# Region attention on one core: where a region's two evacuations of turned probabilities and its first turn stand in the order of ScalarE and TensorE

## The chip, the cores and the metric

The kernel runs on one core of one Trainium2 chip. The metric is device time in microseconds (us), the median of several runs. The core has TensorE (PE, which multiplies and turns matrices and writes to PSUM), ScalarE (ACT), VectorE (DVE), GpSimd (POOL) and SyncE (SP, which issues DMAs). Each engine works through its own instructions in order, and semaphores join them.

## What is computed

The input is a batch of 8 images of 56x56 tokens with 256 channels, f32. After a group norm, a 1x1 projection gives queries, keys and values. Each image is cut into 7x7 = 49 regions of 64 tokens. Each region chooses 4 regions by the product of mean queries and mean keys, and attends to their 256 keys with 8 heads of 32 channels. A depthwise 3x3 convolution of the values is added, a 1x1 projection follows, and the input is added.

```python
qkv = einsum('nchw,oc->nohw', group_norm(x), qkv_w) + qkv_b
a_r = pool(q) @ pool(k)                 # 49 x 49 for each image
idx = top_k(a_r, 4)                     # four key regions for each query region
attn = softmax(q * 256**-0.5 @ gathered_k.T)   # 8 heads, 64 queries, 256 keys
out = attn @ gathered_v + depthwise3x3(v)
y = x + (einsum(out, out_w) + out_b)
```

## The kernel before

**The loop.** After a start of 89 us that projects the first image, the loop runs over 56 rows of regions (`s`, 7 rows an image) and the 7 regions of a row (`rc`); `r = 7 s + rc` numbers 392 regions. Every engine has its own copy of this loop with its own order, written by hand. Beside the attention of the present regions, a row's seven passes carry the projections of the row seven rows later (values `v`, keys `k`), of queries two rows later, the turned values (`vt`), the output projection of the row before, the 16 taps of the convolution on VectorE, and the statistics of an image two ahead. The last seven rows have no `v`, `k` and `vt` left to project. The first row of an image also chooses its regions, and the last row of an image also settles a later image's statistics.

**One region.** It goes through these steps; the eight heads are four slices of PSUM (`u` = 0 to 3), with two heads on the two halves of the partitions.

- `scores` (PE, L907 to L920): 16 matmuls on tiles of 32x64 into `s_bank`, one bank for each `u`. There is one set of these four banks, so the scores of the next region wait until all four exponentials of this one are done.
- `maximum` (DVE, L697): two reductions, each over two banks.
- `exp` (ACT, L495): four activations into `probs`, of which there is one copy. Exponentials 0 and 1 of a region wait for the first turn of the region before, 2 and 3 for its second.
- `turn_probs(r, 0)` and `turn_probs(r, 1)` (PE, L923): four transposes each, of two slices, into `pt_bank`. This is one bank, so each turn waits until the last one was evacuated.
- `probs_t_out(r, 0)` and `(r, 1)` (ACT, L504): the two evacuations of `pt_bank` to `probs_t`, a copy of 128x512 each.
- `attend` (PE, L935): 32 matmuls on tiles of 128x32 with the selected values. It waits for both evacuations of its region.
- `turn_recips` (PE, L952), `recips_out` (ACT, L510), `normalize_o` (DVE, L713), `take_region` (POOL, L332): the sums' reciprocals are turned and evacuated, the result is scaled and added to the convolution.

**The order on TensorE in pass `r`** (L990 on): first turn of `r`; wait for the exponentials of `r`; the image's small matmuls where there are any; scores of `r + 1`; attend of `r - 1`; second turn of `r`; projections; `turn_recips(r)`; more projections.

**The order on ScalarE in pass `r`** (L537 on): first evacuation of `r`; one or two evacuations of the row's projections (`q_out`, `v_out`, `k_out`, `vt_out`), called the row's evacuations here; exponentials 0 and 1 of `r + 1`; second evacuation of `r`; exponentials 2 and 3 of `r + 1`; `recips_out(r)`.

```python
pe.wait_ge(probs_t_evac, 2 * r + hf)            # turn_probs: the bank is free
act.wait_ge(probs_turned, 2 * r + hf + 1)       # probs_t_out: the turn is done
act.wait_ge(probs_turned, 2 * (r - 1) + u // 2 + 1)   # exp, u = 0 and 2
pe.wait_ge(exp_done, HG * (r + 1))              # before the scores of r + 1
pe.wait_ge(probs_t_evac, 2 * r + 2)             # attend
```

Of the kernel before, what the change touches and what calls it, by code (L numbers as in the profile page):

```python
# [21 lines left out]
HG = P // HD  # L22
# [34 lines left out]
def is_row(n):  # L57
    return 0 <= n < ROWS


def is_region(r):
    return 0 <= r < ALL
# [40 lines left out]
def attention_kernel(nc, x, w_qkv, w_out, b_qkv, b_out, w_tap, b_tap, ident_d, group_d, v_dram, out):  # L103
    place, early_chunks = chunk_places()

    with ExitStack() as ctx:
# [340 lines left out]
        def _(act):  # L447
# [30 lines left out]
            def q_out(n, k):  # L478
                if not is_row(n):
                    return  # L480
                if n >= Q_RING:
                    act.wait_ge(scores_done, NWIN * (n - Q_RING + 1))
                wait_full(act, "q", n, k)
                act.activation(q_all[:, n % Q_RING, k, :, :].rearrange("p g (r c) -> p r g c", r=RS),  # L484
                               by_image(bank_of("q", n, k)[:, 0:ROW]), ACT.Identity,
                               bias=bq_scaled[:, k:k + 1], scale=SCALE).then_inc(free("q", n, k), 1)
# [8 lines left out]
            def exp(r, u):  # L495
                act.wait_ge(max_done, 2 * r + u // 2 + 1)
                if u % 2 == 0 and r:
                    act.wait_ge(probs_turned, 2 * (r - 1) + u // 2 + 1)
                if u == 0 and r >= 2:
                    act.wait_ge(inv_done, r - 1)  # L500
                act.activation(probs[:, u, :], s_bank[:, u, 0:KEYS], ACT.Exp, bias=neg_max[:, r % 2, u:u + 1],  # L501
                               accum_out=denom[:, r % 2, u:u + 1]).then_inc(exp_done, 1)

            def probs_t_out(r, hf):  # L504
                act.wait_ge(probs_turned, 2 * r + hf + 1)
                if r >= 2 and hf == 0:
                    act.wait_ge(attn_done, r - 1)
                act.copy(probs_t[:, r % 2, hf, :], pt_bank[:, :]).then_inc(probs_t_evac, 1)  # L508
# [27 lines left out]
            for s in range(STEPS):  # L536
                kv, first, last_row = s + KV_LEAD, s % NWIN == 0, s % NWIN == LAST  # L537
                for rc in range(NWIN):
                    r = s * NWIN + rc
                    if is_region(r):  # L540
                        probs_t_out(r, 0)

                    if rc == 0:
                        if first and s:
                            q_out(s - 1 + Q_LEAD, 0)
                        if s:
                            q_out(s - 1 + Q_LEAD, 1)
                    elif rc == 1:
                        v_out(kv, 0)
                    elif rc == 2:  # L550
                        v_out(kv, 1)
                    elif rc == 3:
                        k_out(kv, 0)
                    elif rc == 4:
                        k_out(kv, 1)
                        if last_row:
                            vt_out(kv, 0)
                    elif rc == 5:
                        vt_out(kv, 1 if last_row else 0)
                    elif not last_row:  # L560
                        vt_out(kv, 1)
                        q_out(s + Q_LEAD, 0)

                    if is_region(r + 1):
                        exp(r + 1, 0)
                        exp(r + 1, 1)
                    if is_region(r):
                        probs_t_out(r, 1)
                    if is_region(r + 1):
                        exp(r + 1, 2)  # L570
                        exp(r + 1, 3)
                    if rc == 1 and first and is_row(kv):
                        qk_means_out(kv // NWIN)
                    if is_region(r):
                        recips_out(r)
# [256 lines left out]
        def _(pe):  # L832
# [90 lines left out]
            def turn_probs(r, hf):  # L923
                if r or hf:
                    pe.wait_ge(probs_t_evac, 2 * r + hf)
                else:
                    pe.wait_ge(chunk_free[5], early_chunks[5])
                pe.wait_ge(exp_done, HG * r + 2 * hf + 2)
                for u in (2 * hf, 2 * hf + 1):
                    for c in range(CH):  # L930
                        at = P * (CH * (u % 2) + c)
                        t = pe.transpose(pt_bank[:, at:at + P], probs[:, u, P * c:P * (c + 1)], ident[:])  # L932
                t.then_inc(probs_turned, 1)
# [54 lines left out]
            for s in range(STEPS):  # L988
                xr, kv, qn = s + STAT_LEAD, s + KV_LEAD, s + Q_LEAD
                first, last_row = s % NWIN == 0, s % NWIN == LAST  # L990
                for rc in range(NWIN):
                    r = s * NWIN + rc
                    if is_region(r):
                        turn_probs(r, 0)
                        pe.wait_ge(exp_done, HG * (r + 1))

                    if rc == 1 and first and is_row(kv):
                        region_means(kv // NWIN)
                    elif rc == 2 and first and is_row(kv):
                        affinities(kv // NWIN)  # L1000
                    elif rc == 3 and first and is_row(kv):
                        pe.wait_ge(aff_taken, kv // NWIN + 1)
                    elif rc == 2 and last_row and is_row(xr):
                        group_means(xr // NWIN)
                    elif rc == 3 and last_row and is_row(xr):
                        group_vars(xr // NWIN)
                    elif rc == 4 and last_row and is_row(xr):
                        pe.wait_ge(var_eps, xr // NWIN + 1)

                    if is_region(r + 1):  # L1010
                        scores(r + 1)
                    if is_region(r - 1):
                        attend(r - 1)
                    if is_region(r):
                        turn_probs(r, 1)

                    if rc == 0:
                        project("v", kv, 0, 0, 4)
                    elif rc == 1:
                        project("v", kv, 1, 1, 4)  # L1020
                    elif rc == 2:
                        project("k", kv, 0, 2, 4)
                    elif rc == 3:
                        project("k", kv, 1, 3, 4)
                        if last_row:
                            turn_v(kv, 0)
                        else:
                            project_out(s - 1, 0, 0, 2)
                    elif rc == 4:
                        if last_row:  # L1030
                            turn_v(kv, 1)
                            project_out(s - 1, 0, 0, 2)
                        else:
                            project_out(s - 1, 1, 0, 4)
                    elif rc == 5:
                        if last_row:
                            project_out(s - 1, 1, 0, 4)
                        else:
                            turn_v(kv, 1)
                            project("q", qn, 0, 0, 2)  # L1040
                    else:
                        if last_row:
                            project("q", qn, 0, 2, 4)
                            project("q", qn, 1, 0, 2)
                        else:
                            project("q", qn, 1, 0, 2)

                    if is_region(r):
                        turn_recips(r)

                    if rc == 0:
                        project("v", kv, 1, 0, 1)
                    elif rc == 1:
                        project("k", kv, 0, 0, 2)
                    elif rc == 2:
                        project("k", kv, 1, 0, 3)
                    elif rc == 3:
                        if not last_row:
                            project_out(s - 1, 0, 2, 4)
                    elif rc == 4:  # L1060
                        if last_row:
                            project_out(s - 1, 0, 2, 4)
                        else:
                            turn_v(kv, 0)
                    elif rc == 5:
                        if last_row:
                            project("q", qn, 0, 0, 2)
                        else:
                            project("q", qn, 0, 2, 4)
                    else:  # L1070
                        project("q", qn, 1, 2, 4)
# [29 lines left out]
```

## Time and profile before

| what | value |
|---|---|
| median of 3 runs | 1802.1 us (1801.96 to 1802.63) |
| the profiled execution's own time | 1803.27 us |
| its span in the trace | 1801.4 us |
| granted TensorE clock, mean over the span | 0.991 of full speed |
| TensorE, matmuls | busy 1708.4 us (95%) |
| TensorE, weight loads | busy 1384.0 us (77%) |
| VectorE | busy 1517.6 us (84%) |
| ScalarE | busy 1466.7 us (81%) |
| GpSimd | busy 1097.6 us (61%) |
| the chain that ended last | 70% TensorE, 15% ScalarE, 9% VectorE, 4% issue |

The span is the time between the first and the last instruction on the core; the execution's own time has some 2 us around it. A timeline row gives the start, the time of the whole merged group, the engine, the line, and in brackets how long the engine sat idle before and who ended it. Matmuls overlap, and their ends are modelled, so the distance between two starts says more than a duration. PE stands for matmuls and PEld for weight loads.

### The profile page before, as it was taken

How to read it: one execution, taken by the hardware profiler on the slowest of the kernel's cores; microseconds unless marked ns; L12 is line 12 of the kernel's file. 1: busy time of each engine (PE TensorE's matmuls, PEld its weight loads, DVE VectorE, ACT ScalarE, POOL GpSimd, SP SyncE). 2: the span in 40 equal slices, each digit the busy share in tenths (PEclk: the TensorE clock that was granted, in tenths of full speed). 3: DMA queues.
4: the chain of work that ended last, by engine and by line, in shares of the span. 5: the costliest groups of instructions: out<-in, count | busy, mean ns of one | idle time of the engine just before them, and what ended most of it. 6: DMA issues, size and time to landing. Idle time of an engine off the chain costs nothing.

```text
span 1801.4 us, 76163 instructions
## 1 busy us (share of the span) xinstructions
PE 1708.4 (95%) x26568; PEld 1384.0 (77%) x26568; DVE 1517.6 (84%) x3329; ACT 1466.7 (81%) x4793; POOL 1097.6 (61%) x2464
## 2 busy tenths in 40 slices
PE   4999999999999999999999999999999999988886
PEld 4878887888878887788878888788887888766664
DVE  6478988898988898898888898889897888888884
ACT  1478888888878888788888888788887888877775
POOL 3256666666656666666666666666665666555542
PEclk9999999999999999999999999999999999999999
DMA  5323434343434444344443343434343434332332
GB/s 183 87 83 109 145 113 136 102 137 115 143 100 127 125 127 123 116 130 124 128 121 120 117 137 116 130 105 145 107 134 89 119 103 123 97 116 87 105 95 84
DMA packets 157016, 211.66 MB, mean 117 GB/s; under 512 B 17888, under 2 KB 144736, under 8 KB 156640
## 3 DMA queue, kind: packets, MB, share of 16 engines
q1 hardware_dynamic: 141408, 129.71, 24.9%
q0 software_dynamic: 15232, 77.08, 12.9%
q8 instruction: 219, 3.59, 0.9%
q14 instruction: 157, 1.29, 0.2%
HBM read 155.33 MB, written 51.38 MB: 115 GB/s over the span
## 4 chain that ended last, share of the span: by engine, by line
PE 70%; ACT 15%; DVE 9%; issue 4%; DMA 0%; POOL 0%; ACTq 0%; POOLq 0%; DVEq 0%
PE chunk_bank L848 20%; PE pt_bank L932 15%; PE s_bank L919 12%; ACT probs L501 11%; PE o_bank L946 9%; PE chunk_bank L862 8%; DVE neg_max L699 4%; DVE lepe L603 3%; PE chunk_bank L877 2%; PE o_bank L956 2%; ACT probs_t L508 2%; ACT v_stage L475 1%; ACT q_all L484 1%; PE s_bank L848 1%; PE s_bank L895 1%
## 5 line engine op out<-in xcount | busy, mean ns | idle before, releaser
L501 ACT ACTIVATE probs<-s_bank,neg_max 128x256 f32<-128x256 f32 x1568 | 737.4, 482 | 190.2 <-DVE neg_max L699 189.9
L699 DVE TENSOR_REDUCE neg_max<-s_bank 128x2 f32<-128x512 f32 x784 | 506.0, 685 | 158.0 <-PE s_bank L919 157.0
L328 POOL COPY k_sel<-k_all 128x128 f32 x1568 | 403.9, 299 | 377.0 <-PE s_bank L919 354.9
L603 DVE SCALAR_TENSOR_TENSOR lepe<-v_band,taps,lepe 128x448 f32<-128x448 f32 x896 | 608.4, 725 | 0.0
L848 PE MATMUL chunk_bank<-xn,wqkv 128*128 128x224 f32 x2544 | 570.6, 357 | 2.5 <-DVE xn L639 2.5
L508 ACT COPY probs_t<-pt_bank 128x512 f32<-128x512 f32 x784 | 464.5, 593 | 71.2 <-PE pt_bank L932 70.5
L932 PE MATMUL pt_bank<-ident,probs 128*128 128x128 f32 x3136 | 498.1, 282 | 11.8 <-ACT probs_t L508 11.6
L848 PEld LDWEIGHTS chunk_bank<-xn,wqkv 128*128 128x128 f32 x2544 | 442.6, 192 | 11.7 <-DVE xn L639 2.6
L932 PEld LDWEIGHTS pt_bank<-ident,probs 128*128 128x128 f32 x3136 | 358.5, 141 | 70.9 <-ACT probs_t L508 19.0
L339 POOL TENSOR_TENSOR lepe<-o_norm,lepe 128x128 f32<-128x128 f32 x392 | 255.3, 651 | 187.3 <-DVE o_norm L717 186.8
L501 ACT ACTIVATION_READ_ACCUMULATOR probs<-s_bank,neg_max 128x1 f32 x1568 | 330.6, 211 | 0.0
L946 PEld LDWEIGHTS o_bank<-probs_t,v_sel 128*32 128x32 f32 x12544 | 195.2, 110 | 152.6 <-issue 152.0
L919 PE MATMUL s_bank<-k_sel,q_all 32*64 32x256 f32 x6272 | 272.0, 402 | 20.1 <-ACT probs L501 10.8
L946 PE MATMUL o_bank<-probs_t,v_sel 128*32 128x64 f32 x12544 | 258.9, 223 | 1.0 <-ACT recips_t L512 0.6
L862 PE MATMUL chunk_bank<-lepe,wout 128*128 128x224 f32 x896 | 194.0, 353 | 1.0 <-POOL lepe L339 1.0
L346 POOL TENSOR_SCALAR lepe<-v_band,taps,btap 128x448 f32<-128x448 f32 x112 | 169.1, 1510 | 0.0
L862 PEld LDWEIGHTS chunk_bank<-lepe,wout 128*128 128x128 f32 x896 | 159.9, 190 | 3.5 <-POOL lepe L339 1.2
L919 PEld LDWEIGHTS s_bank<-k_sel,q_all 32*64 32x64 f32 x6272 | 92.3, 130 | 90.8 <-ACT probs L501 49.6
L956 PE MATMUL o_bank<-ident,recips 128*128 128x128 f32 x392 | 108.7, 277 | 18.3 <-DVE o_norm L717 18.3
L710 DVE COPY recips<-rdenom 128x128 f32<-128x128 f32 x392 | 104.5, 267 | 13.5
L694 DVE SCALAR_TENSOR_TENSOR resid<-chunk_bank,bout,resid 128x448 f32<-128x448 f32 x112 | 76.0, 678 | 47.3 <-PE chunk_bank L862 47.3
L512 ACT COPY recips_t<-o_bank 128x128 f32<-128x128 f32 x392 | 113.4, 289 | 0.0
(69 smaller groups left out, 1196.1 us busy)
## 6 DMA issues: line engine op xcount, KB each, us to landing
v_sel<-v_dram SPq DMA_DIRECT2D x1568, 64.0 KB
xn<-x_dram POOLq DMA_DIRECT2D x56, 448.0 KB, 4.9
v_dram<-v_stage SPq DMA_DIRECT2D x112, 224.0 KB
resid<-x_dram POOLq DMA_DIRECT2D x56, 448.0 KB, 4.3
out_dram<-resid POOLq DMA_DIRECT2D x56, 448.0 KB, 3.3
wqkv<-w_qkv_dram SPq DMA_DIRECT2D x1, 768.0 KB, 9.8
wout<-w_out_dram SPq DMA_DIRECT2D x1, 256.0 KB, 12.4
idx_row<-top_idx SPq DMA_DIRECT2D x8, 0.8 KB
```

Source lines behind the costliest of these rows:

```text
L328: last = pool.tensor_copy(k_sel[:, r % K_SLOTS, :, RT * j:RT * (j + 1)], k_all[:, b % 2, :, bass.ds(reg[j] * RT, RT)])
L339: pool.tensor_tensor(cells, o_norm[:, r % 2, :].rearrange("p (k r c) -> p k r c", k=KC, r=RS), cells, ALU.add).then_inc(o_row_done, 1)
L346: pool.tensor_scalar(in_image(lepe[:, k, n % LEPE_RING, :]), v_band[:, n % BANDS, k, 1:1 + RS, 1:1 + W], taps[:, k, MID_TAP:MID_TAP + 1], ...
L501: act.activation(probs[:, u, :], s_bank[:, u, 0:KEYS], ACT.Exp, bias=neg_max[:, r % 2, u:u + 1], accum_out=denom[:, r % 2, u:u + 1]).then_ ...
L508: act.copy(probs_t[:, r % 2, hf, :], pt_bank[:, :]).then_inc(probs_t_evac, 1)
L603: ins = dve.scalar_tensor_tensor(row, v_band[:, n % BANDS, k, t // 3:t // 3 + RS, t % 3:t % 3 + W], taps[:, k, t:t + 1], row, ALU.mult, AL ...
L699: dve.tensor_reduce(neg_max[:, r % 2, 2 * hf:2 * hf + 2], s_bank[:, 2 * hf:2 * hf + 2, 0:KEYS], AX.X, ALU.max, negate=True).then_inc(max_d ...
L848: ins = pe.matmul(bank_of(kind, n, k)[:, cols], wqkv[:, part, col:col + P], xn[:, part, n % X_RING, cols], start=(part == 0), stop=(part = ...
L862: ins = pe.matmul(bank_of("out", g, m)[:, cols], wout[:, part, P * m:P * (m + 1)], lepe[:, part, g % LEPE_RING, cols], start=(part == 0), ...
L919: last = pe.matmul(s_bank[RT * k:RT * (k + 1), u, 0:KEYS], q_all[s, g % Q_RING, k, rc, :], k_sel[s, r % K_SLOTS, k, :], start=True, stop=True)
L932: t = pe.transpose(pt_bank[:, at:at + P], probs[:, u, P * c:P * (c + 1)], ident[:])
L946: last = pe.matmul(o_bank[HD * u:HD * (u + 1), RT * k:RT * (k + 1)], v_sel[:, r % V_SLOTS, c, HD * head:HD * (head + 1)], probs_t[:, r % 2 ...
```

## The change

On ScalarE, the first evacuation moves behind the row's evacuations, and the second moves behind all four exponentials of the next region. So the four exponentials follow each other, with one evacuation ahead of them and one behind. On TensorE, the first turn moves from the head of the pass to the place between the scores of the next region and the attend of the last one. No instruction is added or taken away, and no wait changes its count.

```diff
@@ scalar @@
                 for rc in range(NWIN):
                     r = s * NWIN + rc
-                    if is_region(r):
-                        probs_t_out(r, 0)
-
                     if rc == 0:
...
                         vt_out(kv, 1)
                         q_out(s + Q_LEAD, 0)

+                    if is_region(r):
+                        probs_t_out(r, 0)
                     if is_region(r + 1):
-                        exp(r + 1, 0)
-                        exp(r + 1, 1)
+                        for u in range(HG):
+                            exp(r + 1, u)
                     if is_region(r):
                         probs_t_out(r, 1)
-                    if is_region(r + 1):
-                        exp(r + 1, 2)
-                        exp(r + 1, 3)
@@ tensor @@
                     if is_region(r):
-                        turn_probs(r, 0)
                         pe.wait_ge(exp_done, HG * (r + 1))
...
                     if is_region(r + 1):
                         scores(r + 1)
+                    if is_region(r):
+                        turn_probs(r, 0)
                     if is_region(r - 1):
                         attend(r - 1)
```

## Rows read from the trace of the kernel before

**Rows 1.** The page: busy time by engine, and TensorE's granted clock in 40 slices
```profile
PE 1708.4 (95%) x26568; PEld 1384.0 (77%) x26568; DVE 1517.6 (84%) x3329; ACT 1466.7 (81%) x4793; POOL 1097.6 (61%) x2464
...
PEclk9999999999999999999999999999999999999999
```
**Rows 2.** Busy time in one stretch: start:end, length, then each engine, clock, DMA
```profile
950.00:1250.00 300.00, 296.07 (x4662) 242.36 (x4651) 263.31 (x579) 257.48 (x845) 197.31 (x435) 1.00 0.40 121
```
**Rows 3.** Timeline of a middle row's pass rc = 4: start, us, engine, line, work
```profile
902.89 0.60 PE L932 MATMUL pt_bank<-ident,probs 128*128 128x128 f32 x4
...
903.42 0.69 PE L919 MATMUL s_bank<-k_sel,q_all 32*64 32x256 f32 x16
903.53 0.58 ACT L508 COPY probs_t<-pt_bank 128x512 f32<-128x512 f32 x1 [0.24 <-PE pt_bank L932]
...
904.04 0.65 PE L946 MATMUL o_bank<-probs_t,v_sel 128*32 128x64 f32 x32
904.22 1.29 DVE L699 TENSOR_REDUCE neg_max<-s_bank 128x2 f32<-128x512 f32 x2
...
904.62 0.66 PE L932 MATMUL pt_bank<-ident,probs 128*128 128x128 f32 x4
904.94 0.47 ACT L501 ACTIVATE probs<-s_bank,neg_max 128x256 f32<-128x256 f32 x1 [0.29 <-DVE neg_max L699]
...
905.86 0.58 ACT L508 COPY probs_t<-pt_bank 128x512 f32<-128x512 f32 x1
906.32 0.49 ACT L501 ACTIVATE probs<-s_bank,neg_max 128x256 f32<-128x256 f32 x1
...
906.74 0.60 PE L877 MATMUL chunk_bank<-ident,v_band 128*114 128x128 f32 x4
906.78 0.49 ACT L501 ACTIVATE probs<-s_bank,neg_max 128x256 f32<-128x256 f32 x1
...
907.18 0.60 PE L932 MATMUL pt_bank<-ident,probs 128*128 128x128 f32 x4
...
907.71 0.69 PE L919 MATMUL s_bank<-k_sel,q_all 32*64 32x256 f32 x16
```
**Rows 4.** Timeline where the program starts: a second turn with no attend before it
```profile
96.00 0.58 ACT L508 COPY probs_t<-pt_bank 128x512 f32<-128x512 f32 x1
...
96.62 0.42 PEld L932 LDWEIGHTS pt_bank<-ident,probs 128*128 128x128 f32 x4 [0.60 <-ACT probs_t L508]
```
**Rows 5.** Timeline, passes rc = 6 and 0 of two middle rows, scores and last turn
```profile
977.32 0.69 PE L919 MATMUL s_bank<-k_sel,q_all 32*64 32x256 f32 x16
...
980.64 0.60 PE L932 MATMUL pt_bank<-ident,probs 128*128 128x128 f32 x4
...
981.39 0.69 PE L919 MATMUL s_bank<-k_sel,q_all 32*64 32x256 f32 x16
...
985.63 0.69 PE L919 MATMUL s_bank<-k_sel,q_all 32*64 32x256 f32 x16
```
**Rows 6.** Timeline of TensorE in the first row of an image, pass rc = 1
```profile
954.98 0.69 PE L919 MATMUL s_bank<-k_sel,q_all 32*64 32x256 f32 x16
...
959.83 0.35 PE L903 MATMUL s_bank<-qk_mean 128*49 128x49 f32 x4 [0.55 <-ACT qk_mean L491]
```
**Rows 7.** Timeline in the last row of an image: rc = 1 on TensorE, 5 on VectorE
```profile
1138.49 0.35 PE L885 MATMUL s_bank<-mv,group 128*128 128x2 f32 x2 [0.29 <-DVE mv L645]
...
1154.06 1.28 DVE L699 TENSOR_REDUCE neg_max<-s_bank 128x2 f32<-128x512 f32 x2
```
**Rows 8.** Timeline in the last seven rows: two starts of scores, the exponential between
```profile
1707.28 0.69 PE L919 MATMUL s_bank<-k_sel,q_all 32*64 32x256 f32 x16 [0.27 <-ACT probs L501]
...
1710.64 0.49 ACT L501 ACTIVATE probs<-s_bank,neg_max 128x256 f32<-128x256 f32 x1
...
1711.27 0.69 PE L919 MATMUL s_bank<-k_sel,q_all 32*64 32x256 f32 x16 [0.27 <-ACT probs L501]
```
**Rows 9.** Busy time of one region there, columns as in the windows above
```profile
1735.60:1740.10 4.50, 4.00 (x57) 2.68 (x57) 3.42 (x8) 3.31 (x12) 1.82 (x5) 0.58 0.25 67
```

## The prediction

> **What bounds the kernel now.** I read the page first. TensorE is busy for 95% of the span, VectorE for 84%, ScalarE for 81%, and the granted clock stands at full speed in nearly every slice [rows 1]. In 300 us in the middle it is 296 of 300 us [rows 2]. The page's mean hides little here, since the stages of a row repeat.
>
> Then I read the timeline of one pass in the middle of an image [rows 3]. All times from here on are counted from the start of the scores at 903.42. TensorE goes scores 0, attend 0.62, second turn 1.20, projections, the last four transposes of values until 3.92, the next first turn 3.76, the next scores 4.29. No gap lies between these. ScalarE ends the last exponential at 3.85 (906.78 + 0.49), 0.44 before the next scores. So the scores do not wait for it: this pass is bound by TensorE's own instructions, at 4.29 us.
>
> The other limit is the circle scores, maximum, four exponentials, next scores. It closes where TensorE has little to do, in the last seven rows: 1707.28 to 1711.27 is 3.99 us, and there the scores follow the start of the last exponential by 0.63 [rows 8]. In pass rc = 6 of a middle row this circle sets the end too: the first turn starts at 980.64 and would let the scores go 0.53 later as in rows 3, at 981.17, but they start at 981.39; the pass takes 4.07 us. The next, rc = 0, takes 4.24 [rows 5]. The other passes of a middle row are like the one of rows 3.
>
> **The change part by part.** Nothing is added or removed, so every term is a wait or a change of neighbours.
>
> *The first turn behind the scores.* The second turn needs the bank that the first filled, so it waits for the first evacuation. Before, scores and attend lay between (1.73 us from the first turn's start at -0.53 to the second's at 1.20), and the copy from 0.11 to 0.69 was hidden with 0.5 to spare. Now only the attend lies between. Step by step: the first turn starts at 0.62, where the attend started; after matmuls on other tiles a turn takes 0.66 (the second turn of rows 3), so it ends at 1.28. The copy follows a turn's end by 0.04 (903.49 to 903.53) and takes 0.58, until 1.90. TensorE follows the end of such a copy by 0.04 to 0.05: 96.58 to 96.62 [rows 4], a place in the old trace where no attend stood between and the turn did wait. So the second turn starts at 1.95 instead of 1.20, and all behind it moves by 0.75.
>
> *The head of the pass.* Without the first turn there, the scores follow the projections. In rows 3 different tiles overlap by 0.07 (turn end 904.11 is 0.07 after the next start, likewise scores to attend and attend to turn), equal tiles by 0.16 (transposes of values end 907.34, turn starts 907.18). The work that ended at 3.92 ends at 4.67, and the next scores start at 4.60 instead of 4.29. The pass grows by **0.31 us**: 0.16 is waiting (the attend, started 0.07 before 1.28 and 0.65 long, would let the turn go at 1.79, not 1.95), 0.15 the order of the work, with four meetings of unlike tiles in place of three and a first turn that takes 0.66 and not 0.60. That a project is followed by scores, scores by a turn, and a turn by an attend at the same 0.07 is taken from their nearest neighbours in rows 3; the bounds are nothing extra (0.16 in all) and 0.1 more for a switch that overlaps nothing (0.41).
>
> The Trainium skill has a rule that speaks against the change here: in TensorEngine Tiling (Array Packing), Key Properties, changing the tiling mode drains TensorE. By it the fourth meeting costs something on top of the wait; the two overlaps above agree in direction. By the rule the sum is the one below, without it that of the second case.
>
> *Four exponentials in one run.* The copy between them costs 0.46 of the circle now (905.86 to 906.32). After the change the first exponential follows the first copy by that 0.46, at 1.78; the maximum is ready at 1.52 and no longer decides. The fourth starts three times 0.46 later, at 3.16, and scores are possible at 3.79, 0.2 earlier than 3.99. Behind TensorE's 4.60 that is worth nothing. Exponential 2 needs the second turn, done at 2.61, and is due at 2.70: a margin of 0.05 to 0.09. If it is missed, ScalarE's slack of 0.8 hides it except in the last rows.
>
> *The second copy behind the run.* The next first turn and the next attend wait for it. It ends at 4.20 at the latest, they start at 5.22 and 5.81: hidden. `recips_out` and the row's evacuations follow (0.29 and up to 0.6 + 0.65) and end by 5.8 in rc = 6, where there are two; the next first copy is due at 5.92. Hidden by 0.1; what a late one would cost stands in the range. The projections' banks are freed earlier than before. VectorE's maxima start where they did. No DMA is moved; SP's loads of values wait for the attend, which ends 0.6 later, and have more than two passes to land; POOL's gathers wait for the scores, as before.
>
> *The sum.* A middle row: six passes at +0.31, and rc = 6, which loses the 0.22 it waits now, +0.09; 1.95. There are 35: **+68 us**. First rows of an image: rc = 1 waits on ScalarE for the means [rows 6], which the run brings 0.2 forward and the copy that is now ahead of them puts 0.46 back, +0.26; five others at +0.31 and rc = 6 at +0.09; 1.9 by 7: **+13**. Last rows: rc = 1 and 2 wait for VectorE's statistics, [rows 7], 0 and -0.2; rc = 5 has its maximum late at 1154.06, so the removed copy gives 0.46 back; rc = 3 gains 0.2 by the shorter circle, and rc = 4 then finds ScalarE late, +0.6; rc = 0 and 6 +0.31. Together 0.3 by 7: **+2**. Last seven rows: passes without projections gain 0.2 to 0.46, the four with eight matmuls lose 0.18 (4.17 for 3.99): about **-3**, with 0 to -8 as its bounds, since some passes there run part of their time at the lower level of the clock now (0.58 of full speed granted over one of 4.50 us, [rows 9]; the levels are 1.2 and 2.4 GHz) and may or may not still do so.
>
> That is +80 on the profiled execution: span 1801.4 to 1881, own time 1803.3 to 1883. The median of the runs is 1.2 below that execution, so I take **1882**.
>
> **The rivals.** *Only the wait counts:* the order costs nothing, 0.16 a pass. 35 by 0.90, 7 by 1.0, the last rows of images -2, the end -5: +32, **1834**. For it: ends of matmuls are modelled, so an overlap of 0.07 or 0.16 may be partly drawn. Against: start to start shows the same.
>
> *The copy hides under the attend:* slower by nothing, and then faster by the circle. The attend takes 0.65; the copy with both hand-overs 0.67. If attend's 32 weight loads spread to 0.75 behind a turn, no wait is left and the pass stays at 4.2; rc = 6 gives back 0.22 (35 rows, 7.7), the last rows of images 5, the end 12: -25, **1777**. It decides at a wait under some 0.03 a pass. Against it: the attend's start is tied to the turn's end, and so is the copy's; and an attend that is longer by 0.1 costs TensorE that 0.1.
>
> *ScalarE comes late everywhere:* if the row's evacuations end after the turn, the first copy and all behind it wait; 0.1 in each of 300 passes is +30, **1912**. For it: 0.1 to spare in rc = 6. Against: 0.8 in the rest.
>
> *No effect:* TensorE's waits land in slack I took for work. Against it: 296 of 300 us busy; **1802**.
>
> **How the numbers follow.** Forecast 0.70 (with the order at 0.31 and its bounds), only the wait 0.18, ScalarE late 0.06, hidden copy 0.03, no effect 0.03. The range holds the forecast, the second case and the third: the wait alone less 4, 1830, up to 0.41 a pass, 300 passes by 0.1 more, some 1915. Within 0.2% (3.6 us, about what a measurement of this kernel can tell from none) takes the no-effect case, 0.03; faster 0.03; slower 0.94.
>
> **What would show it.** Right: in a middle row scores start every 4.55 to 4.6 us, the second turn's weight load shows idle time ended by the evacuation in nearly every pass, the last exponential ends 0.8 before the next scores, and ScalarE waits for the first turn. The order's share is the time from the last projection to the scores and from scores to turn. Wrong: second turns that start at 1.8 or earlier; scores that still follow the last exponential by 0.63; first copies that start later than 0.04 behind the turn.

## The result, and the profile after

| | before | after |
|---|---|---|
| median of the runs | 1802.0 us (4 runs) | 1875.0 us (1873.3 to 1875.4, 4 runs) |
| ratio, 95% interval | | 1.040 (1.0385 to 1.042) |
| profiled execution, span | 1801.4 us | 1872.9 us |

The kernel became slower by 73 us, where 80 were forecast (1882, range 1830 to 1915). The page of the changed kernel, busy times:

```profile
PE 1763.3 (94%) x26568; PEld 1358.3 (73%) x26568; DVE 1520.7 (81%) x3329; ACT 1464.3 (78%) x4793; POOL 1091.5 (58%) x2464
```

Every engine has the instructions of before [rows 1]. ScalarE's and VectorE's busy time is within some 3 us of what it was; TensorE's matmuls are drawn 55 us longer and its weight loads 26 us shorter, for the same work. So TensorE's share of 94% does not show that it waits more than before. The sum of waits of the changed kernel does (engine, line, whom it waited for; total, times, longest):

```profile
ACT probs_t L508 <- PE pt_bank L928: 303.3, 386, 2.5
...
PEld pt_bank L928 <- ACT probs_t L508: 117.9, 434, 0.9
```

ScalarE waited 70.5 us in 230 places for a turn before, 303.3 in 386 now; TensorE's weight loads of a turn waited 19.0 us in 33 places for an evacuation, 117.9 in 434 now. The two engines hand a bank to and fro, and each sits still while the other has it. The busy times of the middle stretch of the changed kernel show it on the weight loads and on ScalarE (columns as in [rows 2]):

```profile
950.00:1250.00 300.00, 291.94 (x4420) 225.20 (x4415) 250.41 (x560) 242.35 (x797) 183.78 (x410) 1.00 0.39 117
```

In the same 300 us 4420 matmuls ran instead of 4662 [rows 2], 5% fewer, at the same clock.

One pass, rc = 4 of a middle row, the timeline of the changed kernel, to be read beside [rows 3]:

```profile
1043.97 0.69 PE L915 MATMUL s_bank<-k_sel,q_all 32*64 32x256 f32 x16
...
1044.59 0.66 PE L928 MATMUL pt_bank<-ident,probs 128*128 128x128 f32 x4
...
1045.17 0.65 PE L942 MATMUL o_bank<-probs_t,v_sel 128*32 128x64 f32 x32
1045.18 1.28 DVE L695 TENSOR_REDUCE neg_max<-s_bank 128x2 f32<-128x512 f32 x2
1045.28 0.58 ACT L508 COPY probs_t<-pt_bank 128x512 f32<-128x512 f32 x1 [0.94 <-PE pt_bank L928]
1045.90 0.47 ACT L501 ACTIVATE probs<-s_bank,neg_max 128x256 f32<-128x256 f32 x1
1045.91 0.42 PEld L928 LDWEIGHTS pt_bank<-ident,probs 128*128 128x128 f32 x4 [0.25 <-ACT probs_t L508]
1045.92 0.65 PE L928 MATMUL pt_bank<-ident,probs 128*128 128x128 f32 x4
...
1047.26 0.48 ACT L501 ACTIVATE probs<-s_bank,neg_max 128x256 f32<-128x256 f32 x1
...
1047.71 0.60 ACT L508 COPY probs_t<-pt_bank 128x512 f32<-128x512 f32 x1
...
1048.03 0.60 PE L873 MATMUL chunk_bank<-ident,v_band 128*114 128x128 f32 x4
...
1048.56 0.69 PE L915 MATMUL s_bank<-k_sel,q_all 32*64 32x256 f32 x16
```

Counted from the scores at 1043.97: first turn 0.62, attend 1.20, copy 1.31 to 1.89, second turn 1.95, last exponential done 3.77, next scores 4.59. The pass takes 4.59 instead of 4.29. ScalarE sat idle for 0.94 before the copy, and the weight load of the second turn for 0.25 after the attend's last.

The times of all passes, from the starts of the scores in the two timelines (medians over the middle rows of the images, and of the rows that stand apart):

| pass rc = | 0 | 1 | 2 | 3 | 4 | 5 | 6 | row |
|---|---|---|---|---|---|---|---|---|
| middle rows, before | 4.24 | 4.24 | 4.29 | 4.23 | 4.29 | 4.29 | 4.07 | 29.65 |
| middle rows, after | 4.54 | 4.54 | 4.54 | 4.54 | 4.60 | 4.60 | 4.16 | 31.52 |
| first row of an image, before | 6.32 | 5.13 | 4.40 | 4.23 | 4.28 | 4.29 | 4.07 | 32.73 |
| first row of an image, after | 6.26 | 5.41 | 4.54 | 4.54 | 4.60 | 4.60 | 4.16 | 34.11 |
| last row of an image, before | 4.24 | 4.89 | 4.95 | 3.99 | 4.29 | 5.25 | 4.71 | 32.31 |
| last row of an image, after | 4.54 | 4.89 | 4.66 | 3.78 | 4.79 | 5.29 | 4.92 | 32.88 |
| most of the last seven rows, before | 4.41 | 3.99 | 3.99 | 3.99 | 3.99 | 3.99 | 3.99 | 28.35 |
| the other three, rc = 1 and 2 at 0.56 to 0.70 of the clock | 4.41 | 4.47 | 4.76 | 3.99 | 3.99 | 3.99 | 3.99 | 29.59 |
| the last seven rows, after | 3.78 | 3.79 | 3.79 | 4.17 | 4.16 | 4.16 | 4.16 | 28.01 |

The first 49 rows together took 1491.5 us before and 1570.3 after, +78.8; the last seven 193.9 and 187.1, -6.9. The start ahead of the first row is 1.2 us shorter, the end behind the last scores 0.8 longer. That is the 71.5 us between the spans. The pass rc = 6 of [rows 5] is that of a first row of an image; middle rows have the same 4.07.

### The profile page after: what moved, and what is told of

Same layout as the page of the kernel before. It is cut to its first block, busy times and chain, and to the rows that moved or that the text cites. A ratio compares the mean times of both kernels' runs of the same rounds, so it can differ in the third digit from the quotient of the medians.

```text
span 1872.9 us, 76163 instructions
## 1 busy us (share of the span) xinstructions
PE 1763.3 (94%) x26568; PEld 1358.3 (73%) x26568; DVE 1520.7 (81%) x3329; ACT 1464.3 (78%) x4793; POOL 1091.5 (58%) x2464
## 4 chain that ended last, share of the span: by engine, by line
PE 79%; ACT 16%; issue 3%; DVE 1%; DMA 0%; POOL 0%; POOLq 0%; ACTq 0%; DVEq 0%
PE chunk_bank L844 25%; PE pt_bank L928 25%; PE s_bank L915 13%; ACT probs_t L508 11%; PE chunk_bank L858 9%; ACT probs L501 4%; PE chunk_bank L873 2%; PE o_bank L952 2%; PE s_bank L844 1%; PE s_bank L891 1%; PE pt_bank L844 0%; DVE stats L616 0%; ACT qk_mean L491 0%; DVE x_sum L625 0%; DMA xn<-x_dram 0%
## 5 line engine op out<-in xcount | busy, mean ns | idle before, releaser
L501 ACT ACTIVATE probs<-s_bank,neg_max 128x256 f32<-128x256 f32 x1568 | 723.8, 476 | 19.9 <-DVE neg_max L695 17.7
L508 ACT COPY probs_t<-pt_bank 128x512 f32<-128x512 f32 x784 | 460.9, 588 | 303.3 <-PE pt_bank L928 303.3
L328 POOL COPY k_sel<-k_all 128x128 f32 x1568 | 397.2, 295 | 420.0 <-PE s_bank L915 398.8
L928 PE MATMUL pt_bank<-ident,probs 128*128 128x128 f32 x3136 | 514.0, 286 | 38.1 <-ACT probs_t L508 2.6
L928 PEld LDWEIGHTS pt_bank<-ident,probs 128*128 128x128 f32 x3136 | 328.3, 140 | 251.9 <-issue 134.1
L501 ACT ACTIVATION_READ_ACCUMULATOR probs<-s_bank,neg_max 128x1 f32 x1568 | 320.8, 205 | 0.0
L706 DVE COPY recips<-rdenom 128x128 f32<-128x128 f32 x392 | 115.3, 294 | 17.4 <-PE o_bank L952 2.6
L713 DVE TENSOR_TENSOR o_norm<-o_bank,recips_t 128x128 f32<-128x128 f32 x392 | 111.3, 284 | 3.7 <-PE o_bank L942 2.5
```

The costliest lines, as they stand in the source:

```text
L328: last = pool.tensor_copy(k_sel[:, r % K_SLOTS, :, RT * j:RT * (j + 1)], k_all[:, b % 2, :, bass.ds(reg[j] * RT, RT)])
```

## The experiments

All eight kernels change the order of the two engines' work or the size of one copy; each ran beside the kernel before, at 1800.5 to 1801.2 us in those comparisons.

**ScalarE's part alone.** The first turn stands ahead of the wait for the exponentials again.

```diff
                     if is_region(r):
+                        turn_probs(r, 0)
                         pe.wait_ge(exp_done, HG * (r + 1))
...
                         scores(r + 1)
-                    if is_region(r):
-                        turn_probs(r, 0)
```

> ScalarE's part of the change alone: the first turn stands at the head of the pass again, the four exponentials stay in one run with a copy ahead and one behind. Theory (one bank for the turns ties the two parts together): the fourth exponential starts 2.90 us after the scores, the copy behind it ends at 3.94, the next first turn needs that copy and so starts at 3.99 instead of 3.70, and the next scores at 4.52: passes of about 4.5 us and 1868 us (1850 to 1885), as slow as the changed kernel although the second turn no longer waits. Rival (the second turn's wait for the first copy is the only cost): passes of 4.2 to 4.3 us as before, some 1795 us.

It took 1939.7 us, 1.077 (1.075 to 1.079) of before. Timeline of a pass rc = 3 of a middle row:

```profile
1053.62 0.69 PE L915 MATMUL s_bank<-k_sel,q_all 32*64 32x256 f32 x16
...
1056.50 0.48 ACT L501 ACTIVATE probs<-s_bank,neg_max 128x256 f32<-128x256 f32 x1
...
1056.95 0.59 ACT L508 COPY probs_t<-pt_bank 128x512 f32<-128x512 f32 x1
...
1057.60 0.42 PEld L928 LDWEIGHTS pt_bank<-ident,probs 128*128 128x128 f32 x4 [0.47 <-ACT probs_t L508]
...
1058.19 0.68 PE L915 MATMUL s_bank<-k_sel,q_all 32*64 32x256 f32 x15
```

The mechanism is the expected one, to some hundredths: last exponential at 2.88, the copy behind it done at 3.92, the first turn at 3.98, the next scores at 4.57. With one bank the copy behind the run of exponentials holds up the next first turn, which stands ahead of the scores. The size of the whole was missed, by 72 us. All seven passes of a middle row take 4.57, also rc = 6 (4.07 before), which the expectation had left out; that is 2.34 a row. The first 49 rows took 104 us more than before. The last seven rows took 229.8 us, 36 more than before: 47 passes of 4.57 make 214.8, and the other 15 us are passes of up to 5.9 where the clock fell below its upper level. Busy times in that stretch,

```profile
1688.00:1918.00 230.00, 181.64 (x2866) 124.18 (x2864) 161.29 (x346) 156.73 (x531) 100.60 (x254) 0.87 0.27 81
```

So the run of exponentials does not go with the old place of the first turn: the two parts of the change belong together.

**TensorE's part alone.** In the kernel before, the first turn goes behind the scores; ScalarE keeps its old order.

```diff
                     if is_region(r):
-                        turn_probs(r, 0)
                         pe.wait_ge(exp_done, HG * (r + 1))
...
                         scores(r + 1)
+                    if is_region(r):
+                        turn_probs(r, 0)
                     if is_region(r - 1):
                         attend(r - 1)
```

> TensorE's part of the change alone: the first turn stands behind the next scores, ScalarE keeps its old order (first copy at the head of the pass, second copy between the exponentials). Theory: the first copy starts 1.31 after the scores, the row's evacuations are stuck behind it, the first exponential starts at 2.4, the fourth at 4.24, and the next scores at 4.87, 5.4 where two evacuations stand in the pass: about 2040 us (2000 to 2070). Rival (only TensorE's order counts, ScalarE's has slack): 1875 us as the changed kernel.

It took 2038.7 us, 1.132 (1.130 to 1.134). Timeline of a middle row's pass:

```profile
1000.59 0.69 PE L919 MATMUL s_bank<-k_sel,q_all 32*64 32x256 f32 x16 [0.18 <-ACT probs L501]
...
1001.90 0.59 ACT L508 COPY probs_t<-pt_bank 128x512 f32<-128x512 f32 x1 [1.21 <-PE pt_bank L932]
1002.38 0.64 ACT L465 ACTIVATE v_band<-chunk_bank,bqkv 128x448 f32<-128x448 f32 x1
...
1002.91 0.48 ACT L501 ACTIVATE probs<-s_bank,neg_max 128x256 f32<-128x256 f32 x1
...
1004.73 0.51 ACT L501 ACTIVATE probs<-s_bank,neg_max 128x256 f32<-128x256 f32 x1
...
1005.38 0.69 PE L919 MATMUL s_bank<-k_sel,q_all 32*64 32x256 f32 x16 [0.18 <-ACT probs L501]
```

ScalarE waits 1.21 for the turn, and the row's evacuation and the copy between the exponentials then lie on the circle: the pass takes 4.79 (4.87 expected), 5.28 in rc = 6. So what the first copy is moved past on ScalarE matters as much as what the first turn is moved past on TensorE.

**The run of four undone.** Only the second copy goes back between the exponentials.

```diff
                     if is_region(r + 1):
-                        for u in range(HG):
-                            exp(r + 1, u)
+                        exp(r + 1, 0)
+                        exp(r + 1, 1)
                     if is_region(r):
                         probs_t_out(r, 1)
+                    if is_region(r + 1):
+                        exp(r + 1, 2)
+                        exp(r + 1, 3)
```

> The changed kernel with the second copy back between exponentials 1 and 2; all else as changed. Theory (TensorE sets the pass, the run of four is worth nothing there): passes of a middle row stay at 4.54 to 4.60, rc = 6 goes from 4.16 to 4.25, the circle in the last seven rows from 3.78 to 4.25: +15 to +20 us, 1892 us. Rival (the run of four shortens every pass by the 0.46 of one copy): 0.3 to 0.46 in each of 392 passes, 1990 us or more.

It took 1909.2 us (1906.4 to 1921.6; the profiled execution 1906.4), 1.063 (1.059 to 1.066); 34 above the changed kernel instead of 15 to 20. Middle rows have passes of 4.54, 4.60 and, in rc = 6, 4.27, as expected: the first 49 rows took 1582.5 us, 12 more than in the changed kernel, of which 7 lie in the last rows of images, where the expectation had none. Timeline of rc = 6:

```profile
1058.77 0.69 PE L918 MATMUL s_bank<-k_sel,q_all 32*64 32x256 f32 x16
...
1061.47 0.59 ACT L508 COPY probs_t<-pt_bank 128x512 f32<-128x512 f32 x1
...
1062.40 0.50 ACT L501 ACTIVATE probs<-s_bank,neg_max 128x256 f32<-128x256 f32 x1
...
1063.04 0.24 PEld L918 LDWEIGHTS s_bank<-k_sel,q_all 32*64 32x64 f32 x16 [0.38 <-ACT probs L501]
```

Here the scores wait for the last exponential again. The last seven rows took 208.6 us at a granted clock of 0.95, where the changed kernel took 187.1 at 1.00: 47 passes of 4.27 make 200.7, and the other 8 us, which the expectation lacked too, are mostly passes rc = 3 of 5.55 and more, partly at the lower level. The run of four is worth its 0.46 to 0.49 only where the circle sets the pass (3.79 becomes 4.27 there).

**The second turn later.** It goes behind the pass's first matmuls of projections, so that these fill the time of the copy. In short, with the rest of each branch behind the turn:

```diff
-                    if is_region(r):
-                        turn_probs(r, 1)
                     if rc == 0:
-                        project("v", kv, 0, 0, 4)
+                        project("v", kv, 0, 0, 1)
...
+                    if is_region(r):
+                        turn_probs(r, 1)
+                    if rc == 0:
+                        project("v", kv, 0, 1, 4)
...
```

> The changed kernel with the second turn behind the pass's first two to four matmuls of projections, which fill the time in which it waited for the first copy. Theory (0.16 waiting and 0.15 order in each pass): passes go from 4.54 and 4.60 to 4.38 and 4.44, 1823 us (1815 to 1835); the order's 0.15 stays. Rival 1 (only the wait costs): 4.23 to 4.29 as before and some 1800 us. Rival 2 (the wait is not on the path): 1875 us.

It took 1841.1 us, 1.023 (1.021 to 1.024): 34 below the changed kernel, 40 above the one before, and slower than the expected 1823 by more than its range. Timeline of rc = 3, TensorE:

```profile
1018.82 0.69 PE L915 MATMUL s_bank<-k_sel,q_all 32*64 32x256 f32 x16
...
1020.02 0.65 PE L942 MATMUL o_bank<-probs_t,v_sel 128*32 128x64 f32 x32
1020.61 0.30 PEld L844 LDWEIGHTS chunk_bank<-xn,wqkv 128*128 128x128 f32 x2
1020.61 0.65 PE L844 MATMUL chunk_bank<-xn,wqkv 128*128 128x224 f32 x2
...
1020.90 0.55 PEld L928 LDWEIGHTS pt_bank<-ident,probs 128*128 128x128 f32 x4
...
1021.09 0.60 PE L928 MATMUL pt_bank<-ident,probs 128*128 128x128 f32 x4
...
1021.53 0.92 PE L858 MATMUL chunk_bank<-lepe,wout 128*128 128x224 f32 x4
...
1023.25 0.47 PE L915 MATMUL s_bank<-k_sel,q_all 32*64 32x256 f32 x8
```

The same work in a pass rc = 3 of the changed kernel:

```profile
1040.63 0.65 PE L942 MATMUL o_bank<-probs_t,v_sel 128*32 128x64 f32 x32
1041.38 0.65 PE L928 MATMUL pt_bank<-ident,probs 128*128 128x128 f32 x4
1041.87 0.54 PE L844 MATMUL chunk_bank<-xn,wqkv 128*128 128x224 f32 x2
1042.25 0.92 PE L858 MATMUL chunk_bank<-lepe,wout 128*128 128x224 f32 x4
```

Nothing waits between the scores at 1018.82 and the next at 1023.25, and the pass still takes 4.43, where 4.54 stood in the changed kernel and 4.23 in the one before. So removing the wait gave back 0.11, and 0.20 stayed. The projection next to the attend is drawn 0.65 long, where it is 0.54 behind the turn in the changed kernel. From the attend's start to the output projection's it is 1.51 here and 1.62 there, of which 0.75 lie between attend and second turn; with the 0.58 of [rows 3] in their place it would be 1.45. So 0.17 of waiting is gone, and this order of the same work costs some 0.06 more than the changed kernel's.

**One more meeting and no wait.** In the kernel before, in rc = 0 to 3, the first two instructions of the projections go between the scores and the attend.

```diff
                         scores(r + 1)
+                    if rc == 0:
+                        project("v", kv, 0, 0, 1)
+                    elif rc == 1:
+                        project("v", kv, 1, 1, 2)
+                    elif rc == 2:
+                        project("k", kv, 0, 2, 3)
+                    elif rc == 3:
+                        project("k", kv, 1, 3, 4)
                     if is_region(r - 1):
                         attend(r - 1)
...
                     if rc == 0:
-                        project("v", kv, 0, 0, 4)
+                        project("v", kv, 0, 1, 4)
...
```

> The kernel before with one more meeting of unlike tiles and no new wait: in the passes rc = 0 to 3 of a row the first matmul of the projections (two instructions) goes between the scores and the attend, so that scores, projection, attend, turn follow each other (four meetings in place of three). Theory (the order of the work costs 0.15 a pass by itself): these passes go from 4.23 and 4.29 to 4.38 to 4.45, 4 passes by 48 rows by 0.15 to 0.2: +29 to +38 us, 1834 us. Rival (only the wait for the copy costs, order is free): 1801 us.

It took 1831.4 us, 1.017 (1.0153 to 1.0187): +30. Timeline of rc = 0, TensorE:

```profile
996.97 0.69 PE L919 MATMUL s_bank<-k_sel,q_all 32*64 32x256 f32 x16
997.59 0.65 PE L848 MATMUL chunk_bank<-xn,wqkv 128*128 128x224 f32 x2
998.16 0.65 PE L946 MATMUL o_bank<-probs_t,v_sel 128*32 128x64 f32 x32
998.75 0.66 PE L932 MATMUL pt_bank<-ident,probs 128*128 128x128 f32 x4
...
1001.40 0.69 PE L919 MATMUL s_bank<-k_sel,q_all 32*64 32x256 f32 x16
```

The pass takes 4.43 instead of 4.24 [rows 5], and so do the other three (4.24, 4.29 and 4.23 before): 0.14 to 0.20 for an order in which nothing waits for another engine. The order is a cost of its own, and the rival of a wait alone is out.

**A longer first copy, in both kernels.** The first copy is made in four pieces.

```diff
-                act.copy(probs_t[:, r % 2, hf, :], pt_bank[:, :]).then_inc(probs_t_evac, 1)
+                n = P if hf == 0 else 2 * CH * P
+                for at in range(0, 2 * CH * P, n):
+                    last = act.copy(probs_t[:, r % 2, hf, at:at + n], pt_bank[:, at:at + n])
+                last.then_inc(probs_t_evac, 1)
```

> The changed kernel with every first copy made in four pieces of 128 columns instead of one of 512, which makes that step longer and nothing else. A copy of 128x128 takes 0.285 us and the next instruction follows it after 0.14 to 0.19, so four end some 0.2 later (0.13 to 0.28) than the one of 0.58. Theory (the second turn waits for the first copy in each pass, and TensorE has nothing else to do): some 370 passes longer by 0.2: 1945 us (1920 to 1975). Rival (the wait is not on the path): 1875 us.

> The same four pieces in the kernel before. Theory (there the copy ends 0.5 before the second turn): nothing in the passes that TensorE sets, 0.2 in rc = 6, where ScalarE is late, and a little in rc = 0: +5 to +15 us, 1811 us. Rival (a longer first copy costs the same in either order): 1875 us.

The changed kernel with it took 1946.1 us, 71 above the changed kernel; the kernel before took 1809.2, 1.005 (1.003 to 1.007) of itself without. Timeline of the changed kernel with the longer copy, in a last row's pass rc = 6:

```profile
1022.71 0.77 ACT L510 COPY probs_t<-pt_bank 128x128 f32<-128x128 f32 x4 [0.73 <-PE pt_bank L931]
1023.53 0.42 PEld L931 LDWEIGHTS pt_bank<-ident,probs 128*128 128x128 f32 x4 [0.44 <-ACT probs_t L510]
```

The copy takes 0.77 in place of 0.58, the second turn starts 0.05 behind its end, and passes of 4.54 become 4.73: all of the 0.19 is on the path. In the kernel before the same 0.19 is hidden in the passes that TensorE sets (4.23 and 4.29 stay) and counts in rc = 6 alone (4.07 to 4.25). There the second turn starts 0.32 behind the end of the longer copy, as this pass rc = 1 shows:

```profile
988.36 0.77 ACT L510 COPY probs_t<-pt_bank 128x128 f32<-128x128 f32 x4 [0.18 <-PE pt_bank L935]
...
989.45 0.66 PE L935 MATMUL pt_bank<-ident,probs 128*128 128x128 f32 x4
```

This shows by itself what the change did: it put the first copy on TensorE's path.

**The changed order where TensorE has little to do.** The kernel before, with the changed order in the last seven rows. `LATE` is 49; each moved line stands twice, once for either order.

```diff
+LATE = ROWS - KV_LEAD
...
                     if is_region(r):
-                        turn_probs(r, 0)
+                        if s < LATE:
+                            turn_probs(r, 0)
                         pe.wait_ge(exp_done, HG * (r + 1))
...
                         scores(r + 1)
+                    if is_region(r) and s >= LATE:
+                        turn_probs(r, 0)
```

> The kernel before with the changed order in its last seven rows alone, where TensorE has little to do and the circle of scores, maximum and exponentials sets the pass. Theory: passes there go from 3.99, 4.41, 4.46 and 4.68 to 3.78 (4.16 where eight matmuls stand in the pass), the lower level of TensorE's clock is gone there, and the rest is as before: 7 us less, 1794.5 us (1792 to 1798). Rival (the shorter circle is worth nothing even there): 1801.5 us.

It took 1795.1 us (9 runs) beside 1800.5 (13 runs), 0.9969 (0.9959 to 0.9979): faster than the kernel before by 0.2 to 0.4%, and so than both. The last seven rows took 187.1 us, as in the changed kernel, and 193.9 before. Busy times of that stretch, first in the kernel before:

```profile
1587.00:1781.00 194.00, 164.98 (x2867) 116.93 (x2865) 159.24 (x345) 150.79 (x528) 100.18 (x254) 0.95 0.32 96
```

and in this one:

```profile
1584.00:1771.00 187.00, 158.32 (x2871) 110.99 (x2863) 160.46 (x344) 151.41 (x529) 100.71 (x254) 1.00 0.33 100
```

The second shows the same work in 7 us less and the upper level of the clock (2.4 GHz) all through, where the first was granted 0.95. The 7 us are not the shorter circle alone. At the upper level the passes without projections go from 3.99 to 3.79, and the four with eight matmuls from 3.99 to 4.17, so that a row gains nothing by the two together. The gain lies in rc = 0, 4.41 before, where VectorE's maxima start 1.23 after the scores in place of 0.80, and in six passes rc = 1 and 2 of 4.46 to 4.80 that ran at 0.56 to 0.70 of the clock before (one is in [rows 9]): 27.7 us, where six of 3.99 make 23.9. A pass rc = 0 and another of the six, in the kernel before (columns as in [rows 2]):

```profile
1731.20:1735.60 4.40, 2.82 (x57) 1.70 (x57) 4.09 (x9) 3.58 (x13) 1.82 (x5) 1.00 0.25 74
...
1740.10:1744.90 4.80, 3.97 (x59) 2.50 (x58) 3.16 (x8) 3.17 (x12) 1.81 (x5) 0.68 0.19 54
```

## Why the prediction was right

*The bound.* TensorE's own instructions set the passes of before, with the scores 0.4 behind the last exponential. Shown: the longer first copy leaves 4.23 and 4.29 as they are in the kernel before, and the run of four, taken away from the changed kernel, leaves rc = 0 to 5 of its middle rows at 4.54 and 4.60. Where the circle is the bound, in the last seven rows, the changed order takes 3.99 to 3.79, as worked out.

*The wait for the first copy.* Each step came out: first turn 0.62 (0.62 forecast), copy 1.31 (1.32) to 1.89 (1.90), second turn 1.95 (1.95). The longer copy shows it on the path after and off it before.

*The order of the work.* Forecast 0.15 of the 0.31 a pass; measured 0.30 in all for rc = 4, 0.31 for rc = 5, 0.25 to 0.31 for the others. The two orders without a wait cost 0.14 to 0.20 more than before, in neighbourhoods a little dearer than the changed kernel's. The rule of the Trainium skill (TensorEngine Tiling (Array Packing), Key Properties) that a change of the tiling mode drains TensorE agrees with that in direction; the runs show 0.14 to 0.20 for one meeting more. How the 0.31 parts into waiting and order in the changed kernel itself follows from the starts of the passes rc = 4. From the attend to the second turn it is 0.75 (1.20 to 1.95) and was 0.58 (904.04 to 904.62 in [rows 3]): 0.17 of waiting. From the transposes of values to the scores it is 0.53 (1048.03 to 1048.56) and was 0.97 with the first turn in between (906.74 to 907.71), 0.44 less; in its new place that turn takes 0.58 (1044.59 to 1045.17): 0.14 for the order. The kernel with the later second turn gave back only 0.11, since its own neighbours cost some 0.06 more.

*Four exponentials in one run, the second copy behind it.* Worth nothing in the middle, as forecast. In rc = 4 the run started at 1.93 and not at 1.78, because the maxima start at 1.21 there in place of 0.80: the working had said that VectorE's maxima start where they did. The slack hid it. ScalarE's evacuations were out of the way: the first copy followed the first turn by 0.03 to 0.04 everywhere but in the last row's rc = 4. There it was late as forecast, at 1.45, and the pass took 4.79 (4.9 forecast).

*The terms that were mis-sized.* The sum for the first 49 rows was 83 and is 78.8. Middle rows: 1.87 a row, 1.95 forecast; rc = 2 gains 0.25 only. First rows: 1.4 for 1.9; rc = 0, with the small matmuls of the means, did not grow (5.91 to 6.33 before, 6.26 after), and rc = 2 gained 0.14 only. Last rows: 0.6 for 0.3, since rc = 5 did not give 0.46 back. VectorE's maxima start there at 2.59 after the scores, where [rows 7] show 2.06, as in this timeline of the changed kernel (scores at 1206.07):

```profile
1206.27 0.68 DVE L690 SCALAR_TENSOR_TENSOR resid<-chunk_bank,bout,resid 128x448 f32<-128x448 f32 x1 [2.43 <-PE chunk_bank L858]
1206.87 1.38 DVE L599 SCALAR_TENSOR_TENSOR lepe<-v_band,taps,lepe 128x448 f32<-128x448 f32 x2
...
1208.66 1.28 DVE L695 TENSOR_REDUCE neg_max<-s_bank 128x2 f32<-128x512 f32 x2
```

The addition behind the output projection and two taps stand ahead of the maxima on VectorE, and the projection's last matmuls are now drawn to 0.07 behind the start of the scores, where they had ended 0.37 ahead of it, as the first turn no longer follows them. The working had moved the projections and had not asked who waits for them. The last seven rows: -6.9 for -3, inside its bounds. At the upper level the passes without projections gained 0.2, and 0.63 in rc = 0 (0.2 to 0.46 forecast), and those with eight matmuls lost 0.18, as forecast; the rest, some 4 us, is that the passes that had run at the lower level no longer did. Whether they would, the working had left open, so that this share lies inside the bounds by luck.

*The rivals.* The hidden copy and no effect fall with the second turn at 1.95. The wait alone falls with the extra meeting. ScalarE late everywhere falls with the copies at 1.31.

## What to carry to other kernels

Two uses of one bank in a pass are a hand-over between engines: ask what the writer does while the bank is being emptied, and put at least as much work there as the copy with both hand-overs takes (0.67 us from the turn's end here, of which the attend covered 0.50). Read which limit sets each pass before shortening one: a shorter circle on ScalarE was worth 0.2 us in the passes where nothing else was the bound, and 7 us in the last seven rows together with the clock, and the place made for it cost 79 us in the 49 rows where TensorE was mostly the bound. A block of work that is moved meets new neighbours, and for matmuls on other tiles that has a price of its own, which shows in the distance from start to start.

## What was not expected of the hardware

- With the clock at its upper level in both, the same two projection instructions are drawn 0.54 behind a turn and 0.65 behind an attend or scores; one meeting of unlike tiles more cost 0.14 to 0.20 us a pass, with no engine waiting for another. The weight loads differ there too: behind other tiles the load is drawn at the same start as its matmul (1020.61 for both), behind the same tile 0.19 ahead of it (1020.90 for 1021.09). That this makes the price is not shown.
- In the last seven rows the granted clock went with the order of the work: 0.95 in the kernel before, 1.00 in the changed one, 0.95 with the copy between the exponentials, 0.87 with ScalarE's part alone. Passes at the lower level took some 4, 0, 8 and 15 us more, in this order, than the same passes at the upper one; why the clock fell in one order and not in another stays open.
- A wait of TensorE that ends under the modelled tail of the matmuls ahead of it is not drawn on the matmul's own row: in the pass shown the second turn has no idle time, its weight load has 0.25, and the wait worked out from the starts is some 0.17.

What stays open: whether two banks for the two turns would take the wait away with the order kept. The kernel's tensors hold eight banks of PSUM as it is, and this was not tried.
